# Attention row maxima two more slots ahead of the scores, keys one more block ahead

## The chip, the cores and the metric

The kernel runs on one core of one Trainium2 chip. The metric is the time of the device for one execution, in microseconds (us). In the rows, PE is TensorE's matrix unit and PEld its weight load, DVE is VectorE, ACT is ScalarE, POOL is GpSimd, and SP is SyncE, whose queue (SPq) issues most of the small transfers.

## The reference, cut to what matters

The program is two transformer layers on 2048 tokens of 128 numbers, each with an attention and an expert feed-forward part. The change is in the first attention:

```
c_q, c_kv = h @ W_DQ + b_DQ, h @ W_DKV + b_DKV        # 32 columns each
q = concat(c_q @ W_UQ + b_UQ, c_q @ W_QR + b_QR)       # 8 heads, 128 + 32
k = concat(c_kv @ W_UK + b_UK, h @ W_KR + b_KR)
attn = softmax(q @ k.T / sqrt(160));  o = attn @ v;  x = x + o @ W_O + b_O
```

The softmax runs over all 2048 keys. The second layer and both feed-forward parts come after it and are the same in both kernels.

## The kernel before

The attention is 32 blocks (NBLK): 8 heads by 4 groups of 512 queries. Block n has 16 key tiles t, taken two at a time in 8 slots. A score product (`scores`, L1480) gives 128 keys by 512 queries in PSUM banks 0 to 2, ScalarE takes the exponential (L630) into the ring `prob`, and TensorE multiplies it by the values (`weigh`, L1524), half a block at a time, in slot 6 and in slot 1 of the next block.

The shift of the softmax is the exact maximum of each query's row. It must be known before the block's first score product, because it enters as one row of `q_cols`. So TensorE also forms the same products the other way round, queries by keys (`half_rows`, L1466), only to take their maxima on VectorE (`chunk_max`, L1058, one 128x512 reduction for each product). A pair `lin` is two such products; a block needs 8 pairs, and the pairs run LEAD = 10 ahead of the score slots. With the last pair of block n+1, in slot 5 of block n, `minus_max(n + 1)` (L1066) reduces the 16 maxima of each query to `nmx`; SP then copies `nmx` into the row of `q_cols` (L493, a transfer of 2 KB in pieces of 4 bytes), and `scores(n + 1, 0)` waits for it (`s_shift`). Slots 6 and 7 lie between.

Row products, key products (`keys`, L1453 and L1454, made by ScalarE in L599 and VectorE in L1044 into `key`), denominators (`totals`, L1537) and outputs (`output`, L1508) share PSUM banks 3 to 6. They take them in turn in the order in which the program lists them (`todo`), so each waits until the item four places before it has been read (`bank_read`). Keys are made KLEAD = 4 blocks ahead, in slot 0. In block 0 there are also queries, values (L1086) and, behind slot 5, `folded` (L1441), which takes the two banks after slot 5's rows.

GpSimd adds the exponentials up for the denominators. In block n: `begin_sum(n, 0)` and `(n, 1)` (L915), `add_pairs(n - 1)` (L929), `begin_sum(n, 2)`, `join_parts(n - 1)` (L933, an adding transfer of 512 KB, written `w_v<-part` in the rows), `begin_sum(n, 3)`, `late_sums(n)` (L921, an adding transfer of 1 MB, `part<-prob`). `add_pairs(n - 1)` waits for the 1 MB transfer of block n-1, and for `totals(n - 2)`. SP also issues, for each block, four small transfers of denominators (L482) ahead of the next `nmx` copy; their source is copied by ScalarE in slot 2.

Of the kernel before, what the change touches and what calls it, by code (L numbers as in the profile page):

```python
# [18 lines left out]
def build_kernel(nc, d, out):  # L19
# [3 lines left out]
    NB = S // BLK  # L23
    C = d["L0_attn_W_DQ"].shape[1]
    H = d["L0_attn_W_QR"].shape[1] // C
# [7 lines left out]
    with ctx:  # L33
# [151 lines left out]
        CPB = NT // 2  # L185
        NBLK = H * NB
# [3 lines left out]
        NG = P // C  # L190
        NW = NT // (2 * NG)
        LEAD = CPB + 2
        KLEAD = NB
        U = 7
        A_BANK = (4, 2)
        KB_AT = H * C1
# [41 lines left out]
        for n in range(NBLK):  # L238
            todo = []
            for slot in range(CPB):  # L240
                lin = CPB * n + slot + LEAD
                if lin < NCHUNK:
                    todo += [("rows", 2 * lin), ("rows", 2 * lin + 1)]
                if slot == 0 and n + KLEAD < NBLK:
                    todo += [("keys", n + KLEAD)] + ([("queries", n + 2)] if n < 2 else [])
                if slot == 5 and n == 0:
                    todo += [("folded", 0), ("folded", 1)]
                if slot == SUMS_AT and 2 <= n < NBLK - 1:
                    todo.append(("sums", n - 2))
                if slot == OUT_AT and 2 <= n < NBLK - 1:  # L250
                    todo.append(("out", n - 2))
            for item in todo:
                place_item(item, 3 + turn % 4)
                turn += 1
# [176 lines left out]
        with nc.Block() as block:  # L431
# [102 lines left out]
            def _(act):  # L534
# [45 lines left out]
                def queries_hi(b, bank):  # L580
                    act.wait_ge(s_cq_ps, b + 1)
                    act.activation(q_rows[:, b, :], ps[:, bank, :], ACT.Identity, bias=unit[:, B_CQM:B_CQM + 1],
                                   scale=unit[:, M_CQ:M_CQ + 1]).then_inc(s_cqh, 1)
# [10 lines left out]
                def keys_hi(e, bank):  # L594
                    h, b = e // NB, e % NB
                    if e == 4 * NB:
                        act.wait_ge(s_kb, 4)
                    act.wait_ge(s_kps, e + 1)
                    act.activation(key[:, h % KBUF, b * BLK:(b + 1) * BLK], ps[:, bank, :], ACT.Identity, bias=kcol_m[:, h:h + 1],  # L599
                                   scale=unit[:, M_KEY:M_KEY + 1]).then_inc(s_kh, 1)  # L600
# [56 lines left out]
                for n in range(NBLK):  # L657
                    for t in range(NT):
                        if t == 4 and n >= 1:
                            sums(n - 1)  # L660
                        if t == 2 * SUMS_AT + 2 and n >= 2:
                            sums_out(n - 2)
                        if t == 10 and n == NBLK - 1:
                            sums_out(n - 1)
                        if t == 2 and n + KLEAD < H * NB:
                            keys_hi(n + KLEAD, BANK["keys", n + KLEAD])
                            if n < 2:
                                queries_hi(n + 2, BANK["queries", n + 2])
                        if t == 12 and n == 0:
                            folded()  # L670
                        exponential(n, t)
                        if n == NBLK - 1 and t == 10:
                            ln0_act(act, 0, 3)
# [334 lines left out]
            def _(dve):  # L1008
# [31 lines left out]
                def keys_lo(e, bank):  # L1040
                    h, b = e // NB, e % NB
                    part_of = key[:, h % KBUF, b * BLK:(b + 1) * BLK]
                    dve.wait_ge(s_kh, e + 1)
                    dve.scalar_tensor_tensor(out=part_of, in0=ps[:, bank, :], scalar=kcol[:, h:h + 1], in1=part_of.bitcast(F32),  # L1044
                                             op0=ALU.add, op1=ALU.subtract).then_inc(s_key, 1)
# [102 lines left out]
                    chunk_max(lin)  # L1148
                for n in range(NBLK):
                    for slot in range(CPB):  # L1150
                        lin = CPB * n + slot + LEAD
                        if lin < NCHUNK:
                            chunk_max(lin)
                        if slot == 0 and n >= 1:
                            add_pair(n - 1, 1)
                        if slot == 1 and n + KLEAD < H * NB:
                            keys_lo(n + KLEAD, BANK["keys", n + KLEAD])
                            if n < 2:
                                queries_lo(n + 2, BANK["queries", n + 2])
                        if slot == 2 and n == 0:  # L1160
                            values()
                        if slot == 5 and n < NBLK - 1:
                            minus_max(n + 1)
                        if slot == OUT_AT and 2 <= n < NBLK - 1:
                            denominators(n - 2)
                            accumulate(n - 2)
                        if slot == 7 and n < NBLK - 1:
                            add_pair(n, 0)
                        if n == NBLK - 2 and slot == 7:
                            ln0_stats(dve, 0)  # L1170
                        if n == NBLK - 1:
                            if slot == 0:
                                ln0_norm(dve, 0)
                            elif slot == 3:
                                denominators(n - 2)
                                accumulate(n - 2)
                                ln0_stats(dve, 1)
                            elif slot == 5:
                                ln0_norm(dve, 1)
                            elif slot == 7:  # L1180
                                denominators(n - 1)
                                accumulate(n - 1)
                                ln0_stats(dve, 2)
# [215 lines left out]
            def _(pe):  # L1399
# [240 lines left out]
                pe.wait_ge(s_wal, 2)  # L1640
                for n in range(NBLK):
                    for slot in range(CPB):
                        lin = CPB * n + slot + LEAD
                        scores(n, 2 * slot)
                        if lin < NCHUNK:
                            bank_read(("rows", 2 * lin))
                            half_rows(lin, 0)
                        scores(n, 2 * slot + 1)
                        if lin < NCHUNK:
                            bank_read(("rows", 2 * lin + 1))  # L1650
                            half_rows(lin, 1)
                        if slot == 0 and n + KLEAD < H * NB:
                            bank_read(("keys", n + KLEAD))
                            keys(n + KLEAD, BANK["keys", n + KLEAD])
                            if n < 2:
                                bank_read(("queries", n + 2))
                                queries(n + 2, BANK["queries", n + 2])
                        if slot == 1 and n == 0:
                            for t in range(3 * TPB, NT):
                                last = values(t)  # L1660
                            last.then_inc(s_val_ps, 1)
                        if slot == 5 and n == 0:
                            bank_read(("folded", 0))
                            bank_read(("folded", 1))
                            folded()
                        if slot == OUT_AT and 2 <= n < NBLK - 1:
                            output(n - 2)
                        if slot == 6:
                            weighted(n, 0)
                        if slot == 1 and n >= 1:  # L1670
                            weighted(n - 1, 1)
                        if slot == SUMS_AT and n >= 2:
                            totals(n - 2)
                        if n == NBLK - 1:
                            if slot == 2:
                                output(n - 2)
                            elif slot == 4:
                                totals(n - 1)
                                bank_read(("norm", 0))
                                ln0_pe(pe, 0, 3)  # L1680
                            elif slot == 7:
                                output(n - 1)
                                last_totals(2)
                                bank_read(("norm", 1))
                                ln0_pe(pe, 1, 4)
                                weigh(n, range(2 * NG, 3 * NG))
                                first_totals()
# [350 lines left out]
```

## Time and profile before

| | us |
|---|---|
| median of 3 runs (lowest, highest) | 775.43 (773.83, 776.80) |
| the profiled execution, its own time | 772.24 |
| its span in the profile | 770.5 |
| VectorE busy, share of the span | 628.7, 82% |
| TensorE busy, share of the span | 725.1, 94% |

The attention's score products run from 37.9 to 517 us of the span. In rows of a timeline the columns are: start, length, engine, line, operation, output<-inputs, shapes, how many were merged (x), and in brackets the idle time of the engine before it and what ended it. Times in the rows are from the span's start.

### The profile page before, as it was taken

How to read it: one execution, taken by the hardware profiler on the slowest of the kernel's cores; microseconds unless marked ns; L12 is line 12 of the kernel's file. 1: busy time of each engine (PE TensorE's matmuls, PEld its weight loads, DVE VectorE, ACT ScalarE, POOL GpSimd, SP SyncE). 2: the span in 40 equal slices, each digit the busy share in tenths (PEclk: the TensorE clock that was granted, in tenths of full speed). 3: DMA queues.
4: the chain of work that ended last, by engine and by line, in shares of the span. 5: the costliest groups of instructions: out<-in, count | busy, mean ns of one | idle time of the engine just before them, and what ended most of it. 6: DMA issues, size and time to landing. Idle time of an engine off the chain costs nothing.

```text
span 770.5 us, 12866 instructions
## 1 busy us (share of the span) xinstructions
PE 725.1 (94%) x4432; PEld 479.0 (62%) x4432; DVE 628.7 (82%) x1273; ACT 463.6 (60%) x1069; POOL 475.7 (62%) x389
## 2 busy tenths in 40 slices
PE   8999999999999999999999999869989999999997
PEld 6655555655655555565555555437656679888885
DVE  7879998998998998998989989724788735877885
ACT  4277666766766666675666766644667760446553
POOL 6456856756765775775666667741669872255674
PEclk9999999999999999999999999989999999999999
DMA  6224475475466456546546645614000000012430
GB/s 148 81 56 83 92 135 104 83 138 110 83 125 124 83 108 119 104 95 118 117 83 117 132 83 110 137 29 114 1 0 2 1 1 1 1 60 78 134 115 28
DMA packets 41673, 64.17 MB, mean 83 GB/s; under 512 B 16380, under 2 KB 25613, under 8 KB 37640
## 3 DMA queue, kind: packets, MB, share of 16 engines
q0 software_dynamic: 12896, 48.76, 32.3%
q1 hardware_dynamic: 27432, 14.48, 7.1%
q8 instruction: 35, 0.57, 0.3%
q10 hardware_dynamic: 1280, 0.12, 0.1%
q14 instruction: 30, 0.25, 0.1%
HBM read 13.35 MB, written 1.10 MB: 19 GB/s over the span
## 4 chain that ended last, share of the span: by engine, by line
PE 45%; DVE 26%; POOL 11%; issue 8%; DMA 8%; ACT 1%; POOLq 0%; ACTq 0%; DVEq 0%
DVE mx L1058 19%; PE ps L1524 10%; PE ps L1466 6%; PE ps L1480 6%; DMA q_cols<-nmx 6%; POOL hid_lo L1004 4%; PE ps L1880 4%; PE ps L1508 3%; POOL nrm L984 2%; DVE pair L1074 2%; PE ps L1920 2%; PE ps L1922 2%; PE ps L1921 2%; PE ps L1537 1%; POOL hid L984 1%
## 5 line engine op out<-in xcount | busy, mean ns | idle before, releaser
L1058 DVE TENSOR_REDUCE mx<-ps 128x1 f32<-128x512 f32 x492 | 307.8, 682 | 40.0 <-PE ps L1466 39.9
L630 ACT ACTIVATE prob<-ps 128x512 f32<-128x512 f32 x512 | 265.6, 618 | 122.7 <-PE ps L1480 116.6
L915 POOL TENSOR_TENSOR part<-prob 128x512 f32<-128x512 f32 x128 | 179.4, 1403 | 119.6 <-ACT prob L630 118.4
L1480 PE MATMUL ps<-q_cols,key 128*128 128x512 f32 x512 | 211.2, 416 | 15.3 <-DMA q_cols<-nmx 14.1
L1466 PE MATMUL ps<-key,q_rows 128*128 128x512 f32 x512 | 208.3, 411 | 4.1 <-DVE key L1044 3.1
L1480 PEld LDWEIGHTS ps<-q_cols,key 128*128 128x128 f32 x512 | 96.2, 189 | 76.8 <-issue 33.2
L1524 PE MATMUL ps<-prob,val 128*32 128x512 f32 x1024 | 124.2, 602 | 0.0
L1466 PEld LDWEIGHTS ps<-key,q_rows 128*128 128x128 f32 x512 | 95.5, 188 | 45.8 <-DVE mx L1058 15.2
L929 POOL TENSOR_TENSOR w_v<-part,pair 128x1024 f32<-128x1024 f32 x31 | 74.3, 2396 | 19.4 <-PE ps L1537 9.8
L1004 POOL TENSOR_TENSOR hid_lo<-hid,hid_hi 128x512 fp32r<-128x512 f32 x44 | 61.5, 1408 | 38.7 <-ACT hid_hi L795 38.7
L1524 PEld LDWEIGHTS ps<-prob,val 128*32 128x32 f32 x1024 | 26.9, 110 | 52.5 <-issue 47.5
L1074 DVE TENSOR_TENSOR pair<-prob 128x512 f32<-128x512 f32 x62 | 54.9, 886 | 0.2 <-ACT prob L630 0.2
L779 ACT ACTIVATE act_g<-ps 128x512 f32<-128x512 f32 x44 | 26.4, 599 | 33.0 <-PE ps L1922 32.7
L606 ACT COPY u_sb<-ps 128x512 f32<-128x512 f32 x32 | 18.8, 587 | 40.0 <-PE ps L1524 40.0
L1106 DVE SCALAR_TENSOR_TENSOR X<-ps,rden,X 128x128 f32<-128x128 f32 x128 | 36.0, 344 | 6.2 <-PE ps L1508 3.0
L747 ACT ACTIVATE pT<-ps 128x128 f32<-128x128 f32 x128 | 33.6, 278 | 12.4 <-PE ps L1857 12.4
L1508 PE MATMUL ps<-proj,u_sb 128*128 128x128 f32 x256 | 36.6, 286 | 2.6
L1365 DVE TENSOR_TENSOR prod<-ps,act_g 128x512 f32<-128x512 f32 x44 | 30.2, 685 | 10.9 <-PE ps L1922 8.7
L921 POOL DMA_DIRECT2D part<-prob x31 | 28.0, 903 | 17.0 <-POOL part L915 16.4
L1508 PEld LDWEIGHTS ps<-proj,u_sb 128*128 128x128 f32 x256 | 31.3, 191 | 11.4 <-DVE mx L1058 11.1
L933 POOL DMA_DIRECT2D w_v<-part x31 | 37.3, 1204 | 0.0
L1920 PE MATMUL ps<-hT_hi,w_hi 128*128 128x512 f32 x88 | 35.5, 403 | 0.0
(284 smaller groups left out, 1128.9 us busy)
## 6 DMA issues: line engine op xcount, KB each, us to landing
part<-prob POOLq DMA_DIRECT2D x31, 1024.0 KB, 7.4
w_v<-part POOLq DMA_DIRECT2D x31, 512.0 KB, 5.0
g_all<-g_rows SPq DMA_DIRECT2D x9, 256.0 KB, 3.5
den<-den_sb SPq DMA_DIRECT2D x124, 0.5 KB, 1.7
g_all<-g_rows SPq DMA_DIRECT2D x6, 224.0 KB, 2.9
X<-in_L_attn_h_t_dram SPq DMA_DIRECT2D x4, 256.0 KB, 4.5
out_dram<-X SPq DMA_DIRECT2D x4, 256.0 KB, 2.8
g_all<-g_rows SPq DMA_DIRECT2D x6, 128.0 KB, 2.8
```

Of the source, the lines that this page charges most:

```text
L630: act.activation(prob[:, g % RING, :], ps[:, g % 3, :], ACT.Exp, scale=SCALE).then_inc(s_exp, 1)
L915: pool.tensor_tensor(part[:, n % 2, g, :], tiles(n, 2 * g, 1)[:, 0, :], tiles(n, 2 * g + 1, 1)[:, 0, :], ALU.add).then_inc(s_sum, 1)
L929: pool.tensor_tensor(fin, part[:, n % 2, bass.ds(0, 2, step=2), :], pair[:, :, :], ALU.add).then_inc(s_sum, 1)
L933: pool.dma_start(fin, part[:, n % 2, bass.ds(1, 2, step=2), :], accum_op=ALU.add).then_inc(s_join, 16)
L1004: pool.tensor_tensor(hid_lo[:, n % 4, :], hid[:, n % 2, :], hid_hi[:, n % 4, :].bitcast(F32), ALU.subtract).then_inc(s_hlo, 1)
L1058: dve.tensor_reduce(mx[:, n % 2, c % TPB, at:at + 1], ps[:, BANK["rows", 2 * lin + j], :], AX.X, ALU.max).then_inc(s_mrd, 1)
L1074: dve.tensor_tensor(pair[:, j, :], prob[:, t % RING, :], prob[:, (t + 1) % RING, :], ALU.add).then_inc(s_pair, 1)
L1466: pe.matmul(ps[:, BANK["rows", 2 * lin + j], :], q_rows[:, k, i * P:(i + 1) * P], key[:, h % KBUF, c0:c0 + BLK], start=True, stop=True).th ...
L1480: pe.matmul(ps[:, g % 3, :], key[:, n // NB % KBUF, t * P:(t + 1) * P], q_cols[:, n % NB, :], start=True, stop=True).then_inc(s_sc, 1)
L1508: last = pe.matmul(ps[:, BANK["out", n], i * P:(i + 1) * P], u_sb[:, n % 2, i * P:(i + 1) * P], proj[:, n // NB, :], start=True, stop=True)
L1524: last = pe.matmul(ps[C * x:C * (x + 1), U, :], val[:, t, :], prob[:, (NT * n + t) % RING, :], start=(t < NG), stop=(t >= NT - NG))
L1920: pe.matmul(out_ps, w[0], x_hi, start=start, stop=False)
```

## The change

Twelve pairs ahead instead of ten: the two further pairs are added in slots 1 and 3 of block 0, which hold two pairs each; `minus_max` moves from slot 5 to slot 3. The keys run five blocks ahead instead of four; block 0 makes two key parts, in slots 0 and 4. The last row products then come in slot 3 of block 30 instead of slot 5, and the last key part in block 26 instead of 27. In all there are as many products, reductions and transfers as before.

```diff
         LEAD = CPB + 2
-        KLEAD = NB
+        AHEAD = 2
+        KLEAD = NB + 1
+        def row_pairs(n, slot):
+            first = CPB * n + slot + LEAD + (min(slot // 2, AHEAD) if n == 0 else AHEAD)
+            count = 2 if n == 0 and slot in range(1, 2 * AHEAD, 2) else 1
+            return [lin for lin in range(first, first + count) if lin < NCHUNK]
+        def key_parts(n, slot):
+            if n == 0 and slot in (0, 4):
+                return [NB + slot // 4]
+            return [n + KLEAD] if slot == 0 and n + KLEAD < H * NB else []
...
# DVE
-                        if slot == 5 and n < NBLK - 1:
+                        for lin in lins[1:]:
+                            chunk_max(lin)
+                        if slot == 5 - AHEAD and n < NBLK - 1:
                             minus_max(n + 1)
...
# PE
+                        for lin in lins[1:]:
+                            for j in range(2):
+                                bank_read(("rows", 2 * lin + j))
+                                half_rows(lin, j)
+                        for e in key_parts(n, slot):
+                            bank_read(("keys", e))
+                            keys(e, BANK["keys", e])
```

The order of banks, ScalarE's and VectorE's key steps follow the same two functions.

## Rows read from the trace of the kernel before

**Rows 1.** The page: the chain that ended last, by line.

```profile
DVE mx L1058 19%; PE ps L1524 10%; PE ps L1466 6%; PE ps L1480 6%; DMA q_cols<-nmx 6%; POOL hid_lo L1004 4%; PE ps L1880 4%; PE ps L1508 3%; POOL nrm L984 2%; DVE pair L1074 2%; PE ps L1920 2%; PE ps L1922 2%; PE ps L1921 2%; PE ps L1537 1%; POOL hid L984 1%
```

**Rows 2.** TensorE's waits: us in total, times, longest.

```profile
PE ps L1480 <- DMA q_cols<-nmx: 14.1, 10, 2.6
PE ps L1466 <- DVE key L1044: 3.1, 11, 0.8
```

**Rows 3.** SP's timeline: issues of the nmx copy.

```profile
94.46 0.53 SPq L493 DMA_DIRECT2D q_cols<-nmx  x1
...
183.13 0.53 SPq L493 DMA_DIRECT2D q_cols<-nmx  x1
199.20 0.53 SPq L493 DMA_DIRECT2D q_cols<-nmx  x1
213.58 0.53 SPq L493 DMA_DIRECT2D q_cols<-nmx  x1
...
464.81 0.53 SPq L493 DMA_DIRECT2D q_cols<-nmx  x1
478.35 0.53 SPq L493 DMA_DIRECT2D q_cols<-nmx  x1
```

**Rows 4.** Transfers in 183.0 to 188.1 us; last column: us to landing.

```profile
q8 instruction: 1, 0.02, 1.2%
...
part<-prob POOLq DMA_DIRECT2D x1, 1024.0 KB, 8.4
q_cols<-nmx SPq DMA_DIRECT2D x1, 2.0 KB, 4.9
```

**Rows 5.** Transfers in 199.1 to 204.2 us, one block later.

```profile
part<-prob POOLq DMA_DIRECT2D x1, 1024.0 KB, 7.0
q_cols<-nmx SPq DMA_DIRECT2D x1, 2.0 KB, 2.7
```

**Rows 6.** VectorE's timeline through one block.

```profile
202.15 1.29 DVE L1058 TENSOR_REDUCE mx<-ps 128x1 f32<-128x512 f32 x2 [0.47 <-PE ps L1466]
...
208.47 4.88 DVE L1058 TENSOR_REDUCE mx<-ps 128x1 f32<-128x512 f32 x8 [0.66 <-PE ps L1466]
213.38 0.17 DVE L1066 TENSOR_REDUCE nmx<-mx 128x4 fp32r<-128x16 f32 x1
213.47 1.28 DVE L1058 TENSOR_REDUCE mx<-ps 128x1 f32<-128x512 f32 x2
```

**Rows 7.** The chain that ended last, 208 to 213 us: start, length, what.

```profile
208.47 3.23 DVE mx L1058 x6
...
212.07 0.69 DVE mx L1058
...
212.81 1.16 PE ps L1508 x8
```

**Rows 8.** All instructions on q_cols: the 32 nmx copies' time to landing.

```profile
DMA to landing us min/median/max: 1.8/3.0/4.9
```

**Rows 9.** VectorE's timeline in block 0.

```profile
45.78 3.67 DVE L1058 TENSOR_REDUCE mx<-ps 128x1 f32<-128x512 f32 x6
```

**Rows 10.** TensorE's timeline: block 0's folded products.

```profile
48.40 1.95 PE L1441 MATMUL ps<-w_o,uvT 128*32 128x128 f32 x64 [0.79 <-DVE mx L1058]
```

**Rows 11.** SP's timeline, 205 to 232 us: denominators' transfers.

```profile
222.27 3.15 SPq L482 DMA_DIRECT2D den<-den_sb  x4
```

**Rows 12.** GpSimd's timeline in blocks 29 to 31.

```profile
487.57 2.40 POOL L929 TENSOR_TENSOR w_v<-part,pair 128x1024 f32<-128x1024 f32 x1 [0.62 <-DMA part<-prob]
...
494.21 0.90 POOL L921 DMA_DIRECT2D part<-prob  x1 [0.54 <-POOL part L915]
...
502.53 2.37 POOL L929 TENSOR_TENSOR w_v<-part,pair 128x1024 f32<-128x1024 f32 x1 [1.12 <-PE ps L1537]
```

**Rows 13.** TensorE's timeline in block 31.

```profile
511.11 1.08 PE L1537 MATMUL ps<-w_v,ones_v 128*32 128x128 f32 x16 [5.83 <-DMA w_v<-part]
```

**Rows 14.** GpSimd's timeline: issue of the 512 KB transfer in the block of rows 6.

```profile
211.28 1.21 POOL L933 DMA_DIRECT2D w_v<-part  x1
```

More of the change, by code:

```diff
@@ L240, in build_kernel @@
             for slot in range(CPB):
-                lin = CPB * n + slot + LEAD
-                if lin < NCHUNK:
+                for lin in row_pairs(n, slot):
                     todo += [("rows", 2 * lin), ("rows", 2 * lin + 1)]
-                if slot == 0 and n + KLEAD < NBLK:
-                    todo += [("keys", n + KLEAD)] + ([("queries", n + 2)] if n < 2 else [])
+                todo += [("keys", e) for e in key_parts(n, slot)]
+                if slot == 0 and n < 2:
+                    todo.append(("queries", n + 2))
                 if slot == 5 and n == 0:
@@ L664, in _ @@
                             sums_out(n - 1)
[L665 to L668, printed above, removed]
+                        if t % 2 == 0 and t >= 2:
+                            for e in key_parts(n, t // 2 - 1):
+                                keys_hi(e, BANK["keys", e])
+                        if t == 2 and n < 2:
+                            queries_hi(n + 2, BANK["queries", n + 2])
                         if t == 12 and n == 0:
@@ L1150, in _ @@
                     for slot in range(CPB):
-                        lin = CPB * n + slot + LEAD
-                        if lin < NCHUNK:
+                        lins = row_pairs(n, slot)
+                        for lin in lins[:1]:
                             chunk_max(lin)
@@ L1155, in _ @@
                             add_pair(n - 1, 1)
[L1156 to L1159, printed above, removed]
+                        for e in key_parts(n, slot - 1):
+                            keys_lo(e, BANK["keys", e])
+                        if slot == 1 and n < 2:
+                            queries_lo(n + 2, BANK["queries", n + 2])
+                        for lin in lins[1:]:
+                            chunk_max(lin)
                         if slot == 2 and n == 0:
                             values()
-                        if slot == 5 and n < NBLK - 1:
+                        if slot == 5 - AHEAD and n < NBLK - 1:
                             minus_max(n + 1)
@@ L1642, in _ @@
                     for slot in range(CPB):
-                        lin = CPB * n + slot + LEAD
+                        lins = row_pairs(n, slot)
                         scores(n, 2 * slot)
-                        if lin < NCHUNK:
+                        for lin in lins[:1]:
                             bank_read(("rows", 2 * lin))
@@ L1648, in _ @@
                         scores(n, 2 * slot + 1)
-                        if lin < NCHUNK:
+                        for lin in lins[:1]:
                             bank_read(("rows", 2 * lin + 1))
                             half_rows(lin, 1)
[L1652 to L1657, printed above, removed]
+                        for lin in lins[1:]:
[5 more added lines that the diff above has]
+                            keys(e, BANK["keys", e])
+                        if slot == 0 and n < 2:
+                            bank_read(("queries", n + 2))
+                            queries(n + 2, BANK["queries", n + 2])
                         if slot == 1 and n == 0:
```

## The prediction

> **What bounds the kernel now.** I began with the page's chain that ended last: VectorE's maxima of row products are its largest line, and the copy of `nmx` into `q_cols` holds 6% [rows 1]. A transfer of 2 KB on the chain is a wait that an earlier issue could remove, so TensorE's waits came next: 14.1 us in ten waits for that copy, the longest 2.6, and 3.1 us in eleven for a key part [rows 2]. The third view is SP's timeline, for the period of a block. From 199.20 to 213.58 it is 14.38 us; of the 25 periods from 94.46 to 464.81, fifteen lie between 14.30 and 14.38, mean 14.33. The one before, from 183.13, is 16.07 [rows 3]. So the wait is not in every block: it comes in about one of three.
>
> The transfers of two neighbouring blocks show why. In the long block the copy landed 4.9 us after its issue, in the next 2.7; in the long one, one packet of the queue that brings instructions ran in the window, and the 1 MB transfer took 8.4 us against 7.0 [rows 4, 5]. I looked at all the long periods: in each from 124 to 450 us such a packet started 2.6 to 2.9 us after the copy's issue. TensorE is ready for the next block about 3.2 us after the issue, so 2.7 to 3.3 us of landing is hidden and 4.7 to 4.9 is not.
>
> Last, what sets 14.33 us where nothing waits. VectorE's timeline has the block: from 202.15 it works until it has read the key part, then 0.66 us pass until TensorE's row product of slot 2 is there, then it does eight reductions in a row [rows 6]. The chain runs through six of them and a seventh (slot 5's first) into TensorE's output products, which need that seventh reduction's bank [rows 7]. So in slots 2 to 5 VectorE leads and TensorE waits for it, 0.4 us a block.
>
> **The sum, part by part.** The counts of products, reductions and copies stay; what changes is where they lie.
>
> *The waits for the copy, steady blocks.* `minus_max` is issued two slots earlier, before four reductions. One reduction follows another every (4.88 - 0.68)/7 = 0.60 us [rows 6], so the copy starts about 2.6 us earlier against the output products, and TensorE wants it some 5.8 us after the issue. The 32 landings reach from 1.8 to 4.9 [rows 8]. The waits go. Their price is the excess of periods: from 94.46 to 464.81 are 370.35 us; 24 blocks at 14.34 and one without a key part at 13.54 (464.81 to 478.35) [rows 3] make 357.7. Gain **12.65 us**, including the 0.2 us that a key part is late after each wait. Lower bound of the gain 0, if the copy moves into worse traffic (below).
>
> *minus_max in the middle of VectorE's run.* Now it follows slot 5's second reduction, where VectorE has 0.47 us of idle time coming; later it stands between slot 3 and slot 4, ahead of the seventh reduction. Its price is in the trace: eight reductions from 208.47, the next at 213.47; without `minus_max` the next would have started at 208.47 + 8 x 0.60 = 213.27 [rows 6]. So 0.20 us, although the instruction itself takes little: the next one starts 0.09 us after it, and the rest is that it waits for the reduction before it to end. All of it is ahead of the output products [rows 7]. 25 blocks up to block 28's start: loss **5.0 us**. Bounds: 25 x 0.09 = 2.2 if only the instruction counted, and nothing less, since VectorE is on the chain there; no more than 0.20.
>
> The Trainium skill, "VectorE: DVE Perf Modes", section "The DRAIN you can't avoid", says that a Vector instruction starts only once the pipeline is empty, and that a semaphore between two costs nothing extra. The rows say otherwise for these reductions: they start 0.60 us apart though each lasts 0.68, and lose the overlap at the wait. By the rule the term would be the 2.2 us of the lower bound; I take the row.
>
> *Block 0.* Four more reductions, 4 x 0.60 = 2.4 us; `minus_max` 0.2. `folded` takes two banks after slot 5's rows; with the second key part in slot 4 the item four places before its second bank is that key part, which VectorE reads after slot 5's reductions. So `folded` waits for those two (1.2) and the key step (0.67) too, where it had waited for slot 4 only: VectorE's run of six ends behind it and TensorE already stood 0.79 us for it [rows 9, 10]. And TensorE, held at slot 1's third row product until the queries of slot 0 are read, is late with slot 2's row products, estimated 0.7. Loss **5.2 us**. Bounds: 3.3 (reductions, `minus_max` and key alone) and 6.
>
> *The key part of block 27* moves to block 0. Gain 14.34 - 13.54 = **0.8 us** [rows 3].
>
> *SP's queue.* The four transfers of denominators stand ahead of the copy: 222.27 + 3.15 = 225.42 [rows 11], while the new `nmx` would be ready at about 225.3. Cost to the copy 0.1 to 0.3 us, covered by 0.9 us of slack. What is queued behind the copy there is the next block's denominators, a slot and more later: nothing.
>
> *The end.* In blocks 29 to 31 GpSimd and its transfers are a chain of their own. `add_pairs(29)` at 487.57 waited for the 1 MB transfer; the next was issued at 494.21, landed 7.6 us later, and `add_pairs(30)` began at 502.53 on `totals(29)` instead [rows 12]. So TensorE's 2.6 us wait before block 31 [rows 2] and the rows taken out of block 30 give little: TensorE stands 5.83 us at 511.11 for the last 512 KB anyway [rows 13]. Gain 0.7 us (502.53 against 501.8), less 0.2 us because GpSimd runs closer behind TensorE after a block without a wait: **0.5 us**. Bounds: 0, and 2 if the 1 MB transfers landed in 7.0 instead of 7.5.
>
> Sum: 12.65 - 5.0 - 5.2 + 0.8 + 0.5 = 3.75 us less. The profiled execution took 772.24 with a span of 770.5, so 1.7 lie around it; I expect a span near 766.7. Its time is 3.2 below the median of the runs, so the sum is taken off the median: 775.43 - 3.75 = 771.7, given as **771.6**.
>
> **Rivals.**
>
> *A fetch still catches the copy (slower).* New place: 5.8 us ahead of the next block, so by [rows 3, 14] about 211.1 us, 0.1 us before GpSimd issues the 512 KB transfer at 211.28. Alone, the copy's packets start 1.2 us after the issue and the transfer's data 1.7 after its own. That is 0.3 to 0.5 us of margin. If the copy falls behind, it waits for that data, which ends 4.8 us after its issue, and a fetch adds 1.5. Then it lands 5.3 us after issue, harmless, or 6.8 us, 1.0 late. It decides where the landing passes 5.8 us. With the old wait in all its places the gain of 12.65 is gone: 784.3; with 1.0 in nine blocks 780.6. Against it: three early copies, issued before any such transfer, landed in 1.8 to 1.9 us, the least of [rows 8].
>
> The Trainium skill, "Runtime: NRT & Kernel Launch", section "Instruction fetch mechanics", calls the cost of the fetch at a 16 KB boundary mostly hidden. The packet in [rows 4] stands against that. If it were so, the 4.9 would come from the phase against the 512 KB transfer, and this rival would be likelier.
>
> *VectorE hides the move better.* The insertion costs its own 2.2 and block 0 only 3.3: 771.6 - 2.8 - 1.9 = 766.9. For: the bounds above. Against: the chain names no slack there.
>
> *GpSimd's chain takes over.* After a fetch the 1 MB transfer lands in 8.4 us; then add, two sums and two issues, 13.6 us in all with a landing of 7.0, so 15.0, against a new block of 14.5. It has 0.9 us of slack in other blocks to recover. If it reaches ScalarE's tile 8, 0.5 us return in each of nine blocks, 4.5 in all: 776.1. For: `add_pairs` waits for the transfer in [rows 12]. Against: tile 8 needs the transfer some 9.6 us after its issue.
>
> *Nothing of it shows.* If the waits only move to the next thing late (key parts, [rows 2]), the gain is eaten and block 0 and the insertion remain: 771.6 + 12.65 = 784.3.
>
> **How the numbers follow.** The forecast 0.50, VectorE hides more 0.18, GpSimd's chain 0.16, fetch (whole or in part) 0.12, waits only move 0.04. No change of under 0.5%, 3.9 us, can be told from none for this kernel. My forecast lies on that line: its own range is 769 to 774, and its chance is split between faster (0.28) and same (0.22). VectorE's 0.18 are faster. Of GpSimd's 0.16, 0.13 are same, 0.02 slower, 0.01 faster; of the fetch's 0.12, 0.10 are slower and 0.01 each of the others; of the last 0.04, 0.03 are slower and 0.01 same. So faster 0.48, same 0.37, slower 0.15. Range for 8 in 10: from the low rival at 767 up to 777, which takes in GpSimd's.
>
> **What the profile after would show.** Right: no wait of TensorE for `nmx` in the steady blocks; copies landing near 1.9 us; all periods 14.5 us, where 14.33 and 16.07 alternated; `minus_max` between two reductions 0.80 us apart; block 1's first score product about 5 us later than now (54.3); the last 512 KB wait of TensorE longer than 5.83. Wrong: periods near 14.33 (insertion hidden), periods of 16 (a fetch still hits), ScalarE waiting for GpSimd's transfers, or block 0 growing by 3 us only.

## The result, and the profile after

The median of ten runs after the change is 769.28 us (768.0 to 771.26); that of ten runs of the kernel before, taken beside them, is 773.03 (771.21 to 776.8). The ratio is 0.9944, 95% interval 0.9924 to 0.9965: 3.75 us less were forecast, and 3.75 came. The time itself is 2.3 us under the forecast of 771.6, which stood on a base of 775.43 where ten runs give 773.03. The gain is just over the bound of 0.5%, and the interval reaches to both sides of it. The profiled execution took 768.0 us with a span of 766.3; the span before was 770.5, so the traces differ by 4.2.

The sum can be right with wrong terms, so each term gets its row. First TensorE's waits in the kernel after (us in total, times, longest). The line for `nmx` of [rows 2] is gone, and the last transfer of GpSimd's now heads the list.

```profile
PE ps L1553 <- DMA w_v<-part: 9.5, 1, 9.5
...
PE ps L1496 <- ACT prob L643: 2.2, 4, 1.1
PE ps L1482 <- DVE key L1058: 2.2, 2, 1.6
PE ps L1457 <- DVE key L1058: 2.0, 1, 2.0
```

All instructions on `q_cols`, last line: each of the 32 copies landed 1.9 us after its issue, where [rows 8] had 1.8 to 4.9.

```profile
DMA to landing us min/median/max: 1.9/1.9/1.9
```

SP's timeline: the issues of the copy from block 4's to block 28's.

```profile
97.44 0.53 SPq L506 DMA_DIRECT2D q_cols<-nmx  x1
...
198.96 0.53 SPq L506 DMA_DIRECT2D q_cols<-nmx  x1
213.46 0.53 SPq L506 DMA_DIRECT2D q_cols<-nmx  x1
...
431.02 0.53 SPq L506 DMA_DIRECT2D q_cols<-nmx  x1
444.51 0.53 SPq L506 DMA_DIRECT2D q_cols<-nmx  x1
```

From 97.44 to 431.02 lie 23 periods, 14.50 each; before, 14.33 stood beside 16.07 [rows 3]. The period after that is 13.49: block 27 has no key part now.

VectorE's timeline through the block of 208 to 217 us, for [rows 6]:

```profile
210.75 2.48 DVE L1072 TENSOR_REDUCE mx<-ps 128x1 f32<-128x512 f32 x4 [0.59 <-PE ps L1482]
213.27 0.17 DVE L1080 TENSOR_REDUCE nmx<-mx 128x4 fp32r<-128x16 f32 x1
213.35 3.07 DVE L1072 TENSOR_REDUCE mx<-ps 128x1 f32<-128x512 f32 x5
```

`minus_max` cuts the run after four reductions. Four take 4 x 0.60 = 2.4 us, so the fifth would have started at 213.15; it starts at 213.35, 0.20 us late. The period grows by 0.17 (14.50 against 14.33).

TensorE's timeline in block 0 and at the start of block 1:

```profile
43.38 0.50 PE L1482 MATMUL ps<-key,q_rows 128*128 128x512 f32 x1 [1.58 <-DVE key L1058]
...
46.55 0.63 PE L1496 MATMUL ps<-q_cols,key 128*128 128x512 f32 x1
46.98 0.63 PE L1482 MATMUL ps<-key,q_rows 128*128 128x512 f32 x1
...
53.87 1.96 PE L1457 MATMUL ps<-w_o,uvT 128*32 128x128 f32 x64 [2.05 <-DVE key L1058]
...
59.76 0.40 PE L1496 MATMUL ps<-q_cols,key 128*128 128x512 f32 x1
```

The folded products wait 2.05 us for the key part, in place of 0.79 for a maximum [rows 10], and block 1's first score product is at 59.76, 5.46 later than 54.30. In between the products take 0.63 us instead of 0.40. Stretches of this trace around that place (length, busy time of each engine, granted clock, DMA share and GB/s): the clock is down to its lower level, 1.2 GHz, 2.4 us after TensorE had stood still for 1.58 us. Two later runs with the same stand, `e1_nmx_slot5` and `e6_key_part_slot6` (1.58 and 1.57 us, ended at 43.42 and 43.33), keep the full clock there, so the stand alone does not bring the fall.

```profile
43.00:46.00 3.00, 2.46 (x13) 2.02 (x14) 2.33 (x5) 0.30 (x1) 1.87 (x2) 0.96 0.00 0
46.00:49.00 3.00, 3.00 (x8) 2.32 (x8) 2.84 (x5) 2.09 (x4) 2.04 (x3) 0.50 0.02 5
49.00:52.00 3.00, 2.82 (x11) 1.69 (x10) 2.97 (x7) 2.36 (x5) 1.03 (x1) 0.97 0.02 1
```

Where the 4.2 us of the two spans lie, from the start of the first score product of block n, S(n), in both traces (us, positive is gained):

```
stretch                       before            after             gained
start to S(1)                 54.30             59.76             -5.46
S(1) to S(4)                  98.60 - 54.30     103.24 - 59.76    +0.82
S(4) to S(28)                 454.59 - 98.60    450.31 - 103.24   +8.92
S(28) to the last totals      511.11 - 454.59   507.35 - 450.31   -0.52
from there to the end         770.50 - 511.11   766.30 - 507.35   +0.44
```

Of the +0.82, 0.80 lie between S(3) and S(4) (16.01 us before, 15.21 after): block 4's copy landed 4.1 us after its issue before the change, and 1.9 after it.

### The profile page after: what moved, and what is told of

The parts are those of the page before. It is cut to its first block, busy times and chain, and to the rows that moved or that the text cites. A ratio compares the mean times of both kernels' runs of the same rounds, so it can differ in the third digit from the quotient of the medians.

```text
span 766.3 us, 12866 instructions
## 1 busy us (share of the span) xinstructions
PE 729.1 (95%) x4432; PEld 477.8 (62%) x4432; DVE 623.7 (81%) x1273; ACT 462.6 (60%) x1069; POOL 476.0 (62%) x389
## 4 chain that ended last, share of the span: by engine, by line
PE 59%; DVE 17%; POOL 11%; issue 7%; DMA 3%; ACT 1%; POOLq 0%; ACTq 0%; DVEq 0%
PE ps L1540 14%; DVE mx L1072 12%; PE ps L1496 10%; PE ps L1482 10%; PE ps L1524 5%; POOL hid_lo L1018 4%; PE ps L1900 4%; DMA part<-prob 3%; POOL nrm L998 2%; PE ps L1940 2%; PE ps L1553 2%; PE ps L1942 2%; PE ps L1941 2%; POOL hid L998 1%; PE ps L1469 1%
## 5 line engine op out<-in xcount | busy, mean ns | idle before, releaser
L1482 PE MATMUL ps<-key,q_rows 128*128 128x512 f32 x512 | 212.5, 420 | 3.5 <-DVE key L1058 2.2
L1088 DVE TENSOR_TENSOR pair<-prob 128x512 f32<-128x512 f32 x62 | 48.9, 788 | 0.0
L1381 DVE TENSOR_TENSOR prod<-ps,act_g 128x512 f32<-128x512 f32 x44 | 30.1, 685 | 10.9 <-PE ps L1942 8.6
```

Of the source, the lines that this page charges most:

```text
L1088: dve.tensor_tensor(pair[:, j, :], prob[:, t % RING, :], prob[:, (t + 1) % RING, :], ALU.add).then_inc(s_pair, 1)
L1482: pe.matmul(ps[:, BANK["rows", 2 * lin + j], :], q_rows[:, k, i * P:(i + 1) * P], key[:, h % KBUF, c0:c0 + BLK], start=True, stop=True).th ...
```

## The experiments

Runs with a ratio were timed beside the kernel before on the same chip (773.15, 772.82 and 772.64 us in the three groups). Unless it is said otherwise, an edit is made in the changed kernel. A trace is of one run, whose time can lie some us from the median given.

**The copy back in slot 5.** Only `minus_max` is moved back.

```diff
-    if slot == 5 - AHEAD and n < NBLK - 1:
+    if slot == 5 and n < NBLK - 1:
         minus_max(n + 1)
```

> The kernel after with minus_max back in slot 5; the extra pairs and key part of block 0 stay. My theory: the change's gain comes only from the earlier copy of nmx. So TensorE's waits for the copy come back (10 to 14 us in all, about one block in three, each with an instruction packet 2.6 to 2.9 us after the copy's issue and a landing of 4.7 to 4.9 us), blocks without a wait return from 14.50 to 14.33 us, and block 0 stays 5.5 us longer than before: 777 us, slower than before by about 4.5. Rival (running the pairs twelve ahead is worth something by itself): periods stay near 14.5 with no wait, 769 to 770.

775.62 us (772.92 to 779.06, 12 runs), ratio 1.0036, interval 1.0017 to 1.0054. TensorE's waits:

```profile
PE ps L1496 <- DMA q_cols<-nmx: 10.2, 8, 1.7
PE ps L1553 <- DMA w_v<-part: 8.6, 1, 8.6
```

The waits are back, in eight blocks; blocks without one have a period near 14.33 again (but for block 11, with 15.46, where the clock was at 1.2 GHz for 3.4 us). From S(4) to S(28) it takes 354.98 us for 355.99 before, and the missing key part alone is worth that 1.0. S(1) is 6.7 us later than before (60.97), of which block 1's copy, landing only 6.5 us after its issue, is a part, and the kernel is slower than before: by 2.5 us in the medians, where 4.5 were expected (the spans are 4.5 apart). The lead of the row products and of the keys brings nothing by itself; it only makes room for the early `minus_max`.

**The copy a little earlier, but behind the gate.** Output products wait for a block's seventh reduction, slot 5's first [rows 7]. Here `minus_max` follows directly on it. `chunk_max` got an argument for this, `between`, called after its first reduction.

```diff
-    chunk_max(lin)
+    chunk_max(lin, (lambda: minus_max(n + 1)) if slot == 5 and n < NBLK - 1 else None)
...
-    if slot == 5 - AHEAD and n < NBLK - 1:
-        minus_max(n + 1)
```

> The changed kernel with minus_max inside slot 5, directly behind that slot's first reduction: the seventh one of a block, on which the output products wait. It is then no longer ahead of them, and the copy is issued 0.6 to 0.8 us earlier than in the kernel before, not 2.6. My account: a block in which nothing waits has the period of the kernel before, 14.30 to 14.38 (not 14.50 as in the changed kernel), since the 0.17 us lay only in what stands ahead of the seventh reduction; blocks whose copy meets a fetch packet still wait, about 0.9 us in place of 1.7, so periods of 15.1 to 15.5 in some eight blocks; time 770 to 773, as the copy's earlier issue gives back less than in the changed kernel and the insertion costs nothing. Rival one: the insertion costs VectorE time wherever it lies, so wait-free periods of 14.45 to 14.50, and about 775. Rival two: the copy's delay is not a matter of the packet but of the 1 MB and 512 KB transfers, then an earlier issue of 0.7 us removes all of the delay or none of it.

770.27 us (767.45 to 776.06, 12 runs), ratio 0.9981, interval 0.9959 to 1.0004. TensorE's wait for the copy:

```profile
PE ps L1499 <- DMA q_cols<-nmx: 8.0, 7, 1.6
```

VectorE's timeline, block of 227 us:

```profile
227.83 4.28 DVE L1072 TENSOR_REDUCE mx<-ps 128x1 f32<-128x512 f32 x7 [0.59 <-PE ps L1485]
232.02 0.16 DVE L1082 TENSOR_REDUCE nmx<-mx 128x4 fp32r<-128x16 f32 x1
232.10 1.88 DVE L1072 TENSOR_REDUCE mx<-ps 128x1 f32<-128x512 f32 x3
```

SP's timeline, two issues of the copy without a wait between them and one with:

```profile
217.91 0.53 SPq L506 DMA_DIRECT2D q_cols<-nmx  x1
232.21 0.53 SPq L506 DMA_DIRECT2D q_cols<-nmx  x1
246.52 0.53 SPq L506 DMA_DIRECT2D q_cols<-nmx  x1
262.50 0.53 SPq L506 DMA_DIRECT2D q_cols<-nmx  x1
```

The first half held: 14.30 and 14.31 without a wait, so the insertion costs only ahead of the gate. The second did not: the waits were to shrink from 1.7 to 0.9 us, and the longest is 1.6. The copy is issued 0.6 us earlier against the next block than in slot 5 (3.93 us ahead of its first score product where nothing waits, for 3.33), and of the 10.2 us of waits 8.0 are left. The ratio is 0.0055 lower than with the copy in slot 5 all the same; the traces put 1.1 us of it in block 0, where block 1's copy lands in 1.9 us and not in 6.5, and 2.6 between S(4) and S(28). The order on the queues says why so much of the wait stays. GpSimd's 512 KB transfer and then its 1 MB one, in this kernel:

```profile
216.39 1.21 POOL L947 DMA_DIRECT2D w_v<-part  x1
219.44 0.90 POOL L935 DMA_DIRECT2D part<-prob  x1 [0.54 <-POOL part L929]
```

The copy at 217.91 is 1.52 us behind the 512 KB transfer, and its packets start 2.86 us after the issue, so 4.38 after that transfer's. With the copy in slot 5 the two are 1.84 apart (218.08, 219.92) and the packets start 2.53 after, 4.37; before, 2.30 apart [rows 14, 3], and 2.07 after, 4.37. In these three places the packets start when the 512 KB transfer is through, wherever the issue lies (before, the transfer's last data packet starts at 215.67 us, the copy's first at 215.65). In the changed kernel the order is turned:

```profile
214.01 1.20 POOL L947 DMA_DIRECT2D w_v<-part  x1
```

It comes 0.55 us after the copy (213.46), and the copy's packets start 1.17 to 1.19 us after their issue in every block from 4 on. So rival two of this run is half right: what the lead of 2.6 us bought was the place ahead of that transfer.

**The same two slots early, but without waiting for the reduction in front.** `minus_max` inside slot 4, after that slot's first reduction; it then reads only maxima that are at least one reduction old.

```diff
-    chunk_max(lin)
+    chunk_max(lin, (lambda: minus_max(n + 1)) if slot == 4 and n < NBLK - 1 else None)
...
-    if slot == 5 - AHEAD and n < NBLK - 1:
-        minus_max(n + 1)
```

> The kernel after with minus_max one reduction later: between the two reductions of slot 4 instead of after slot 3's second. The maxima it reads are then complete without waiting for the reduction in front of it to drain. My theory (0.20 us of insertion is 0.09 for the instruction and 0.11 for the wait on the reduction just before): the insertion falls to 0.09, blocks from 14.50 to 14.39 us, 24 steady blocks and a few more give 2.5 to 3 us: 766.5. The copy starts 0.5 us later and still lands in time. Rival (the Trainium skill, VectorE: DVE Perf Modes, section The DRAIN you can't avoid: a semaphore between two instructions costs nothing extra): 14.50 us stays, 769.3.

767.35 us (766.37 to 767.86, 5 runs), ratio 0.9924, interval 0.9905 to 0.9942. VectorE's timeline:

```profile
211.11 3.08 DVE L1072 TENSOR_REDUCE mx<-ps 128x1 f32<-128x512 f32 x5 [0.59 <-PE ps L1485]
214.11 0.16 DVE L1082 TENSOR_REDUCE nmx<-mx 128x4 fp32r<-128x16 f32 x1
214.18 3.08 DVE L1072 TENSOR_REDUCE mx<-ps 128x1 f32<-128x512 f32 x5
```

Five reductions end their turn at 211.11 + 5 x 0.60 = 214.11: now `minus_max` starts at once, and the next reduction 0.07 later. From S(4) to S(28) it takes 344.24 us for 347.07 in the changed kernel, and the period is 14.36 to 14.40 but for one of 14.53 and the last, without a key part, of 13.37. So of the 0.17 us of the changed kernel, 0.12 were the wait for the reduction in front and the rest the instruction. The Trainium skill ("VectorE: DVE Perf Modes", "The DRAIN you can't avoid") has a semaphore after each of a row of vector copies cost nothing extra; the two periods speak against it for this pair. (That section also says that an instruction that is not held starts earlier, so the reductions of 0.68 us that start 0.60 apart are not against it, as the prediction had them.) S(1) is 1.38 us later than in the changed kernel (61.14; the clock was at 1.2 GHz there for 6.8 us, for 3.4), so that S(28) is only 1.62 us earlier (448.69). Then the periods of blocks 29 and 30 grow by 1.4 and 2.0 us, ScalarE waiting 2.04 and 1.37 us for GpSimd's 1 MB transfers, and the last totals start at 507.27, only 0.08 earlier. The rest of the gain in the span (0.7 us) lies behind them, where the granted clock is back at 2.4 GHz at 511.71, in the changed kernel at 513.37. The time of this run is thus partly a matter of that clock, and its interval overlaps that of the changed kernel; the shorter period is what the run shows.

**Block 0: the extra pairs and the key part later.** Extra pairs in slots 6 and 7 of block 0, second key part in slot 6, and block 0's `minus_max` back in slot 5.

```diff
-    first = CPB * n + slot + LEAD + (min(slot // 2, AHEAD) if n == 0 else AHEAD)
-    count = 2 if n == 0 and slot in range(1, 2 * AHEAD, 2) else 1
+    first = CPB * n + slot + LEAD + (max(slot - 6, 0) if n == 0 else AHEAD)
+    count = 2 if n == 0 and slot >= 6 else 1
...
-    if n == 0 and slot in (0, 4):
-        return [NB + slot // 4]
+    if n == 0 and slot in (0, 6):
+        return [NB + slot // 6]
...
-    if slot == 5 - AHEAD and n < NBLK - 1:
+    if slot == (5 if n == 0 else 5 - AHEAD) and n < NBLK - 1:
```

> The kernel after with the two extra pairs of block 0 in slots 6 and 7 instead of 1 and 3, the second key part in slot 6 instead of 4, and block 0's own minus_max in slot 5. VectorE stands idle in those slots of block 0 (1.4 and 1.7 us before the change). My theory: folded no longer waits for the added reductions and the key part, and block 1 starts 1.5 to 2.5 us later than in the kernel before instead of 5.5: 3 to 4 us less than the kernel after, 765.5. Rival (the work is only moved; TensorE or VectorE is late with it in block 1 instead): 769.

766.13 us (765.07 to 767.03, 5 runs), ratio 0.9911, interval 0.9892 to 0.993. S(1) is at 57.54: 2.22 earlier than in the changed kernel and still 3.24 later than before, a little more than expected (1.5 to 2.5). By their count, four extra reductions take 2.4 us of what remains.

**Only the key part later.** The second of those three edits alone.

> The kernel after with only the second key part of block 0 moved from slot 4 to slot 6; the extra pairs stay in slots 1 and 3. My theory: folded then waits for slot 4's reductions alone, as before, and starts 1.9 us earlier (53.87 to 52.0 us of the span; two reductions 1.2 and the key step 0.67); block 1 starts 1.2 to 1.9 us earlier than in the kernel after (59.76), the steady blocks stay at 14.50 us: span near 764.7. Rival (folded is held by VectorE's four added reductions alone): folded stays near 53.9.

767.89 us (one run), span 766.2 against 766.3. TensorE's folded products:

```profile
51.71 1.95 PE L1457 MATMUL ps<-w_o,uvT 128*32 128x128 f32 x64 [0.99 <-DVE mx L1072]
```

They wait for a maximum again, so the step of the prediction about `folded` is shown. They start 2.16 us earlier than in the changed kernel; up to 0.4 of that can be the clock, which stays at 2.4 GHz here. (With the copy back in slot 5 the key part is in slot 4 and the clock is full up to this point; there `folded` waits 2.04 us and starts at 53.45, 1.74 later than here.) S(1) is 1.68 earlier (58.08), but S(4) only 1.01 (102.23), and block 30's period rises from 13.21 to 14.91: nothing is left at the end. Moving the key part alone moves part of the work into block 1 (14.30 for 13.26), and the end is not TensorE's to set.

**Both better places.** Block 0 as above, and `minus_max` inside slot 4 from block 1 on.

> Both edits: extra pairs and key part in slots 6 and 7 of block 0, minus_max inside slot 4 in all blocks but block 0. If the two are independent, their gains add: 2.8 + 3.7 less than the kernel after, 762.8. If GpSimd's chain of sums and transfers (13.6 us a block with a 1 MB transfer that lands in 7.0 us, 15.0 after an instruction packet in it) becomes the bound near 14.4 us a block, less: 765.

764.25 us (762.79 to 767.69, 4 runs; the trace is of the one of 767.69), ratio 0.9878, interval 0.9856 to 0.9901. S(28) is at 445.08, 5.23 earlier than in the changed kernel, yet the last totals begin at 503.54, only 3.81 earlier. ScalarE's timeline in block 29 shows where it went:

```profile
467.35 3.05 ACT L643 ACTIVATE prob<-ps 128x512 f32<-128x512 f32 x6 [2.05 <-DMA part<-prob]
```

ScalarE waits 2.05 us for GpSimd's 1 MB transfer of block 28, which landed 9.2 us after its issue: the exponentials may not overwrite what it still reads. In the changed kernel the two such waits are 1.00 and 1.05 us (485.13, 498.84).

**The end: the 512 KB transfer first.** As the run before, and in block 31 the 512 KB transfer of block 30 is issued directly after its add, ahead of the next sum.

```diff
+    if n == NBLK - 1:
+        join_parts(n - 1)
     begin_sum(n, 2)
-    if n >= 1:
+    if 1 <= n < NBLK - 1:
         join_parts(n - 1)
```

> The kernel of e4_both with one more edit in block 31 alone: GpSimd issues the last 512 KB transfer directly after add_pairs(30), ahead of begin_sum(31, 2). In the chain of the kernel after that sum stands between them with 1.16 us, and TensorE waits 9.5 us for the transfer. My theory (the end is bound by GpSimd's chain): 1.2 us less than e4_both, 763.1. Rival (TensorE or ScalarE bounds the end): the same as e4_both, 764.3.

763.34 us (761.91 to 767.11, 6 runs; the trace is of one of 766.90), ratio 0.9875, interval 0.985 to 0.99. GpSimd's timeline:

```profile
495.07 2.34 POOL L943 TENSOR_TENSOR w_v<-part,pair 128x1024 f32<-128x1024 f32 x1 [1.75 <-DMA part<-prob]
497.71 1.26 POOL L947 DMA_DIRECT2D w_v<-part  x1 [0.30 <-POOL w_v L943]
```

and TensorE's:

```profile
502.75 1.08 PE L1560 MATMUL ps<-w_v,ones_v 128*32 128x128 f32 x16 [8.65 <-DMA w_v<-part]
```

The last totals are 0.8 us earlier than 503.54; 1.2 were expected. This is the lowest median of all, 1.2% below the kernel before; the intervals of this kernel, the one before it and the next overlap, so what the last step is worth in time is not shown, only in the trace.

**The end: block 30's 1 MB transfer before the add.** As the run before, and in block 30 GpSimd makes the sums and issues that transfer first, then `add_pairs(29)` and the 512 KB transfer of block 29.

```diff
+    if n == NBLK - 2:
+        begin_sum(n, 2)
+        begin_sum(n, 3)
+        late_sums(n)
+        add_pairs(n - 1)
+        join_parts(n - 1)
...
```

> The kernel of e8_both_join_first with one more edit in block 30 alone: GpSimd does all four sums and issues the block's 1 MB transfer before it does add_pairs(29) and join_parts(29). The 1 MB transfer then starts when ScalarE's tile 11 is there, some 3 to 4 us earlier, and add_pairs(30) is no longer the end of a row of GpSimd steps. My theory: 2 to 3 us less than e8, until totals(29) bounds add_pairs(30): 760.7. Rival: the transfer of 512 KB of block 29, now issued behind the 1 MB one, lands later by as much as is gained: 763.

764.03 us (762.77 to 766.52, 6 runs), where 760.7 were expected and 763 by the rival; ratio 0.9882, interval 0.986 to 0.9904. GpSimd's timeline:

```profile
483.63 0.87 POOL L935 DMA_DIRECT2D part<-prob  x1 [2.16 <-ACT prob L643]
...
487.20 1.22 POOL L947 DMA_DIRECT2D w_v<-part  x1 [0.30 <-POOL w_v L943]
...
494.60 2.50 POOL L929 TENSOR_TENSOR part<-prob 128x512 f32<-128x512 f32 x2 [4.12 <-DMA w_v<-part]
```

The transfer is issued 4.3 us earlier (483.63 against 487.94), but the 512 KB transfer behind it now lands after 7.3 us instead of 4.9, and GpSimd stands 4.12 us for it. The last totals start at 504.76, 2.0 us later. (The span is 764.2 against 765.2 all the same: the trace of the run before has 10.2 us at 1.2 GHz from 526.6 on, which this one has not; it has 3.4 us from 563.0 on.) The rival held: an earlier issue only changes which of two transfers waits.

**The kernel before with the fetches shifted.** To move TensorE's instruction fetches against the blocks, the kernel before gets 32 one-column products at its start; the attention's work is unchanged.

```diff
+    for _ in range(32):
+        pe.matmul(ps[:, U, 0:1], ident[:, :], ident[:, 0:1], start=True, stop=True)
```

> The kernel before with 32 further one-column products in TensorE's start-up (64 more instructions, their result is overwritten), nothing else. TensorE runs some 256 instructions between two packets of the instruction queue q8 (262 on average), so its packets come a quarter of their 21.9 us period earlier against the program. My theory: a packet that starts 2.6 to 2.9 us after the copy's issue is what makes the copy land at 4.7 to 4.9 us; so the long blocks are no longer n = 6, 10, 14, 17, 21, 24, 28 but others or fewer, and each one still has such a packet at that distance. Start-up adds up to 4 us, so the time says little; the periods do. Rival (the copy's phase against the 512 KB transfer makes it late): the same pattern of long blocks, shifted as a whole at most, without regard to packets.

788.45 us (one run). S(0) is 14.3 us later, where at most 4 were expected (the clock was at 1.2 GHz from 10.9 to 27.9 us), so only the pattern of periods is used. Long blocks (period, from S(n-1) to S(n), over 15.2) from block 5 to block 28, with the starts of the 16 KB fetch packets in us after the issue of the copy for block n (minus is ahead of it), worked out from both traces:

```
before:                          n = 6, 10, 14, 17, 21, 24, 28   fetch at 2.6 to 2.9 in each
shifted: n        5      8      12     15     18     19     26
         period   15.99  15.26  15.97  16.05  15.50  15.82  16.07
         fetch    2.84   -0.34  2.73   2.86   none   2.60   2.87
```

The long blocks moved, and five of seven have their packet at 2.6 to 2.9 us. Two have not, and in one block (n = 23) a packet at 2.52 did no harm; with the copy in slot 5, block 10 was long with a packet at 1.07, and block 25 was not with one at 2.66. So the window as such is not the cause. The copy's own packets show what is. They are 128 of 16 bytes (not of 4, as is said ahead of the prediction), and each eight are followed by one of 4 bytes. DMA queues of the kernel before in block 10, whose copy was issued at 183.13: from 185.20 to 185.97 us, then to 186.92, then to 187.10 (packets, MB, share):

```profile
q1 hardware_dynamic: 135, 0.00, 11.4%
...
q8 instruction: 1, 0.02, 6.3%
...
q1 hardware_dynamic: 9, 0.00, 6.8%
```

120 of the 128 packets go at once, and the last eight only when the fetch is over. Eight of 128 is the share of one of the core's 16 DMA engines. In every long block with a fetch, in all four traces in which the copy is behind the transfer, the last eight come 1.2 to 1.6 us after the others. What counts is the order on that one engine. A fetch that starts just behind the copy's last packet harms nothing (2.30 behind 2.28 in block 7 of the kernel before, 2.52 behind 2.51 in block 23 here, 2.66 behind 2.65 in block 25 with the copy in slot 5); an early one, in block 8 here (-0.34 to 0.90) and in block 10 with the copy in slot 5 (1.07 to 2.02), holds up that engine's part of the 512 KB transfer, and the eight packets with it (1.24 and 1.31 us after the others). Block 18 is the rival's: no fetch is near, but the copy is only 0.92 us behind the 512 KB transfer, for 2.1 to 2.5 in most blocks, so it lands 4.4 us after its own issue and 5.3 after the transfer's, as in a short block (5.2).

## Why the prediction was right

**The waits for the copy: right in mechanism and size.** From S(4) to S(28) 8.92 us were gained; 24 insertions of 0.17 took 4.1 of it, and the missing key part gave 14.50 - 13.49 = 1.0. So the waits were worth 8.9 + 4.1 - 1.0 = 12.0; counted as the prediction does, the same 24 periods give 355.99 - 24 x 14.34 = 11.8. The prediction's 12.65 are for 25 periods; with the one up to S(4) the first sum is 9.72 + 4.25 - 1.0 = 13.0. What the prediction did not see is why the early copy is safe. It held the place near the 512 KB transfer for a danger with 0.3 to 0.5 us of margin; the two runs with a later copy (waits of 10.2 and 8.0 us) show that this place, ahead of the transfer, is most of the gain. The margin was enough: all copies landed in 1.9 us, also with fetches near. Transfers of the changed kernel from 184 to 191 us, last column us to landing:

```profile
q8 instruction: 1, 0.02, 0.9%
part<-prob POOLq DMA_DIRECT2D x1, 1024.0 KB, 8.4
w_v<-part POOLq DMA_DIRECT2D x1, 512.0 KB, 5.5
q_cols<-nmx SPq DMA_DIRECT2D x1, 2.0 KB, 1.9
```

The fetch still lengthens the large transfers (8.4 against 7.0, 5.5 against 4.9), but TensorE waits for neither in that block. "Mostly hidden", as the Trainium skill has it ("Runtime: NRT & Kernel Launch", "Instruction fetch mechanics"), fits this placement; before, such a packet cost TensorE up to 1.7 us (16.02 from S(9) to S(10), for 14.33).

**`minus_max` in VectorE's run: right.** 0.20 was taken, 0.17 of period came, so 4.25 and not 5.0 in 25 periods. The lower bound, 0.09, is nearer to the placement inside slot 4 (14.38 - 14.33 = 0.05) than to this one.

**Block 0: right in sum, one cause missed.** 5.2 forecast, 5.46 measured. The wait of `folded` for the key part is there and goes when the key part is moved. The lower clock from 45.75 to 49.16 was not foreseen. Its cost to `folded` is at most some 0.4 us (53.87, for 53.45 with the copy in slot 5, where the same products ran at the full clock); without the fall block 1 would have begun up to that much earlier.

**The key part: right.** 1.0 came for 0.8.

**The end: the step that failed, by its sign.** "Gain 0.5" from S(28) to the last totals, -0.52 measured. The step took landings of 7.5 and charged 0.2 us for GpSimd's chain running close behind TensorE. The 1 MB transfers of the last blocks landed 8.3, 7.6, 7.6 and 7.0 us after their issue, and GpSimd waited 2.33, 2.81 and 1.74 us for them:

```profile
470.81 2.39 POOL L943 TENSOR_TENSOR w_v<-part,pair 128x1024 f32<-128x1024 f32 x1 [2.33 <-DMA part<-prob]
...
485.10 2.37 POOL L943 TENSOR_TENSOR w_v<-part,pair 128x1024 f32<-128x1024 f32 x1 [2.81 <-DMA part<-prob]
...
498.81 2.34 POOL L943 TENSOR_TENSOR w_v<-part,pair 128x1024 f32<-128x1024 f32 x1 [1.74 <-DMA part<-prob]
```

The start of `add_pairs(30)` is 3.7 us earlier than before, where S(28) was 4.3 earlier. From block 27 on TensorE's blocks have no key part and take 13.49 us, under the 13.6 that the prediction gave GpSimd's chain with a landing of 7.0. The rival "GpSimd's chain takes over" thus sets the end in the last three blocks, and in no steady one; its sign, ScalarE waiting for GpSimd's transfers, came true there (1.00 and 1.05 us in blocks 30 and 31). Every faster version in the experiments pays there too.

**After the attention: two changes of clock that cancel.** TensorE stood 9.49 us before the last totals instead of 5.83 [rows 13], and then ran longer at the lower level. Stretches of the kernel after:

```profile
500.00:505.00 5.00, 0.00 (x0) 0.00 (x0) 2.25 (x12) 0.00 (x0) 5.00 (x6) 0.50 0.19 36
505.00:511.00 6.00, 3.65 (x24) 2.52 (x24) 1.11 (x4) 1.32 (x4) 1.27 (x3) 0.50 0.33 58
511.00:515.00 4.00, 4.00 (x22) 1.35 (x22) 0.18 (x1) 1.88 (x6) 0.00 (x0) 0.70 0.03 4
```

The work between the last totals and the next layer took 1.19 us more for it. In the other direction, the trace before has a stretch at a granted clock of 0.57 from 569 to 573 us, where the one after has 1.00; the rest of the span is 1.63 shorter. Neither was in the sum; together they give the +0.44 of the table. That the clock is the cause of the whole of these two figures is read from the coincidence, not tested.

**The sum.** That it came out to 0.01 us is luck. From S(1) to S(28) 9.7 us were gained where the terms for it give 12.65 - 5.0 + 0.8 = 8.45; the end lost 1.0 more than its term and block 0 0.3 more, and the 0.4 behind the attention was in no term. The traces differ by 4.2 us and the medians by 3.75, an agreement no closer than the runs scatter (768.0 to 771.26).

## What to carry to other kernels

A small transfer on a critical path is worth what stands ahead of it in the shared DMA engines, not what its own issue time says: look for the large transfer next to it and get ahead of that, since an issue 0.6 us earlier but still behind it took away 2.2 of 10.2 us of waits, and one 2.6 us earlier, past it, all. An instruction put into a saturated engine costs least where it reads nothing that the instruction in front has just written, and nothing at all behind the last result that another engine waits for. When a steady state gets faster, look at its last blocks: the chain that had slack in the steady blocks sets the end, and gives back part of each gain.

## What was not expected of the hardware

- A 2 KB copy issued 1.5 to 2.3 us after a 512 KB adding transfer starts its packets only some 4.4 us after that transfer's issue; issued 0.14 us or more before it, they start 1.18 us after their own.
- An instruction fetch (one packet of 16 KB, 0.9 to 1.3 us long) holds up one of 16 DMA engines. If it gets ahead of that engine's eight of the copy's 128 packets, these come 1.2 to 1.6 us after the others, and the copy lands with them (in the kernel before 4.7 to 4.9 us after its issue, instead of 2.7 to 3.3).
- A wait of `minus_max` on the reduction directly in front cost 0.12 us a block (14.50 against 14.38) beside the instruction's own 0.05.
- TensorE's granted clock fell to 1.2 GHz for about 3.4 us (45.75 to 49.16) inside a busy stretch, 2.4 us after a stand of 1.58 us; in two other traces the same stand was followed by no such fall.
- Of two adding transfers of GpSimd's queue, the 512 KB one lands 4.9 us after its issue when it goes ahead of the 1 MB one, and 7.3 after it when it is issued 3.57 us behind (483.63, 487.20).
